# A selective-scan stage whose products with C are summed by accumulating transfers instead of by TensorE

## What is computed

```python
# layer 0
D = sum(adj, axis=1); d = (D + 1e-9) ** -0.5
x = x + relu(((adj * d[:, None] * d[None, :]) @ h) @ W.T + b)        # h = relu(layernorm(x))
# layer 1, after h = layernorm(relu(adj @ h @ gcn_w + gcn_b)) * ln_g + ln_b
dA  = exp(dt[:, :, None] * A[None])                   # (8192, 256, 16)
dBu = dt[:, :, None] * B[:, None, :] * u[:, :, None]
def step(hst, inp):
    dAt, dBut, Ct = inp
    hst = dAt * hst + dBut
    return (hst, hst @ Ct)                            # the sum over the 16 states
y = (ys + u * D_skip) * silu(z)
x = x + y @ w_out
```

## Time and profile before

| | us |
|---|---|
| median of 3 runs | 2683.72 |
| lowest, highest | 2681.23, 2686.16 |
| the profiled execution's own time | 2687.66 |
| its span in the profile | 2685.8 |

### The profile page before, as it was taken

How to read it: one execution, slowest core, us unless ns; L and a number is a source line. 1 busy time by engine, 2 the same in 40 slices (tenths; PEclk the granted TensorE clock), 3 DMA queues, 4 the chain that set the end, 5 groups by cost and what they waited for, 6 DMA issues and landing times.

```text
span 2685.8 us, 22298 instructions
## 1 busy us (share of the span) xinstructions
PE 2325.4 (87%) x7072; PEld 1314.6 (49%) x7072; DVE 2082.0 (78%) x2079; ACT 979.5 (36%) x1696; POOL 936.9 (35%) x409
## 2 busy tenths in 40 slices
PE   0347688999999999999999989999999989997776
PEld 0113344444447888888885444444444444443333
DVE  5888888886645666566652599999999899999997
ACT  0000000000004555555552455555545555555552
POOL 0000000000000000000000388777778788787554
PEclk9978789999999999999999999999999999998898
DMA  8999999898766555555547655555555555551121
GB/s 337 380 398 412 394 393 388 356 404 321 263 247 236 214 214 216 197 213 196 199 183 266 231 198 210 207 208 204 198 211 213 197 207 206 204 196 63 67 75 52
DMA packets 108325, 643.02 MB, mean 239 GB/s; under 512 B 14225, under 2 KB 15025, under 8 KB 42673
## 3 DMA queue, kind: packets, MB, share of 16 engines
q1 hardware_dynamic: 92160, 604.02, 59.3%
q10 hardware_dynamic: 16048, 37.57, 4.0%
HBM read 625.28 MB, written 16.25 MB: 239 GB/s over the span
## 4 chain that ended last, share of the span: by engine, by line
PE 57%; DVE 28%; issue 8%; ACT 3%; ACTq 1%; DMA 1%; DVEq 0%; POOL 0%; SPq 0%; POOLq 0%
PE ps L813 21%; PE ps L731 13%; DVE arena L550 11%; PE ps L853 10%; DVE arena L664 6%; DVE ps L653 6%; PE ps L890 4%; PE ps L928 4%; PE ps L753 2%; ACTq L958 1%; DMA diag_h<-adj 1%; PE ps L874 1%; PE ps L909 1%; DVE ring L664 1%; PE ps L932 1%
## 5 line engine op out<-in xcount | busy, mean ns | idle before, releaser
L813 PE MATMUL ps<-adj_parts,h_parts 128*128 128x512 f32 x2592 | 593.7, 391 | 2.5 <-ACT adj_parts L1024 2.2
L442 POOL TENSOR_TENSOR rstd<-base,minus_half 128x8 f32<-128x8 f32 (+1 forms) x40 | 84.7, 2118 | 1450.7 <-DVE base L490 877.9
L853 PE MATMUL ps<-ring,diag_h 128*128 128x512 f32 x1152 | 549.0, 611 | 0.3 <-DVE arena L640 0.2
L458 POOL TENSOR_TENSOR arena<-arena 128x1024 f32<-128x1024 f32 x192 | 458.5, 2394 | 251.1 <-ACT state L1091 251.1
L813 PEld LDWEIGHTS ps<-adj_parts,h_parts 128*128 128x128 f32 x2592 | 485.0, 188 | 108.6 <-ACT adj_parts L1024 4.7
L550 DVE TENSOR_TENSOR arena<-arena,ring 128x2048 f32<-128x2048 f32 x208 | 476.8, 2292 | 67.0 <-DMA ring<-adj 49.2
L731 PE MATMUL ps<-ring,arena 128*128 128x512 f32 x928 | 437.7, 633 | 62.4 <-DMA ring<-adj 62.4
L664 DVE TENSOR_TENSOR_SCAN arena<-arena,state,ps 128x512 f32<-128x512 f32 x384 | 470.6, 1267 | 26.1 <-DVE ps L653 1.0
L853 PEld LDWEIGHTS ps<-ring,diag_h 128*128 128x128 f32 x1152 | 223.8, 196 | 252.4 <-issue 249.3
L1099 ACT ACTIVATE arena<-arena,a_sb 128x512 f32<-128x512 f32 x512 | 338.3, 708 | 0.4
L577 DVE TENSOR_TENSOR adj_parts<-ring,adj_parts 128x1024 fp32r<-128x1024 f32 x216 | 264.0, 1224 | 94.3 <-ACT adj_parts L1024 83.5
(11 more groups left out here) (85 smaller groups left out, 1783.1 us busy)
## 6 DMA issues: line engine op xcount, KB each, us to landing
ring<-adj SPq DMA_DIRECT2D x480, 1024.0 KB, 6.5
arena<-c_scratch SPq DMA_DIRECT2D x128, 512.0 KB, 3.8
diag_h<-adj SPq DMA_DIRECT2D x32, 1024.0 KB, 12.2
arena<-x ACTq DMA_DIRECT2D x16, 512.0 KB, 4.7
x_scratch<-arena ACTq DMA_DIRECT2D x8, 512.0 KB, 3.0
arena<-x_scratch ACTq DMA_DIRECT2D x16, 256.0 KB, 4.3
out<-arena ACTq DMA_DIRECT2D x16, 256.0 KB, 3.0
lower_scratch<-arena ACTq DMA_DIRECT2D x7, 512.0 KB, 2.6
```

Of the source, the lines that this page charges most:

```text
L458: nc.gpsimd.tensor_tensor(buf, buf, c_row, ALU.mult).then_inc(mult_done, 1)
L813: last = nc.tensor.matmul(acc[:, c, :], h_parts[:, blk % 2, layer, h_part, a * F:(a + 1) * F], adj_parts[:, buf, adj_part, c * MM:(c + 1) ...
L853: last = nc.tensor.matmul((acc_c if i else y_ps)[:, c, :], tile_of(h1, JT * s + a), blk[:, a * STRIP + c * MM:a * STRIP + (c + 1) * MM], s ...
```

## The change

The sum over the 16 states no longer goes through PE pair by pair. There is a buffer y_pair of 128 x 2048 floats (two halves, y_sums[0] and y_sums[1]), paid for by two state buffers: HSB falls from 8 to 6, and the six lie as three pairs. In each chunk:

- POOL's products of slots 0 and 1 are written into y_pair, not in place. POOL waits before slot 0's for PE to have read the previous chunk's y_pair.
- After the product of slots 3, 5, 7, 9, 11 and 13, POOL issues a DMA with accumulate from the pair's buffers (128 x 2048 floats, 1 MB) onto y_pair. Before it issues one it waits for the previous one to have landed. POOL's own addition of pairs (L462 before) is gone.
- PE reads y_pair in slot 16 (the next chunk's slot 0) with four matmuls, after all six transfers have landed; in slot 18 it adds the last pair (slots 14 and 15) from the state buffers with four more. So there are 8 identity matmuls a chunk in all chunks, where there were 16 (32 in the last three).
- A scan that reuses a buffer waits for the product (pair 0), for the landing of its pair's transfer (pairs 1 to 6) or for PE's second sum (pair 7). The skip step on DVE waits for both sums.

```diff
-HSB = 8
+HSB = 6
-NSUM = 6
+YSUM, LAST_PAIR = 16, 18
-SPARED = 3
...
+        hs_pairs = [work2(2 * HALVES * T) for _ in range(HSB // 2 - 1)] + [ring[:, RING - 1, :]]
...
+        y_pair = work2(2 * HALVES * T)
...
+        def added(G):
+            k, p = divmod(G, PAIRS)
+            return 16 * ((PAIRS - 2) * k + min(max(p - 1, 0), PAIRS - 2))
...
-                    nc.gpsimd.tensor_tensor(buf, buf, c_row, ALU.mult).then_inc(mult_done, 1)
-                    if g % 2 and g // 2 < PAIRS_ADDED:
+                    k, n = divmod(g, DS)
+                    if n == 0 and k:
+                        pool.wait_ge(nsum_done, 2 * k - 1)
+                    nc.gpsimd.tensor_tensor(y_sums[n] if n < 2 else buf, buf, c_row, ALU.mult)\
+                        .then_inc(mult_done, 1)
+                    if n % 2 and 2 < n < DS - 2:
                         pool.wait_ge(mult_done, g + 1)
-                        even = hs[(g - 1) % HSB]
-                        nc.gpsimd.tensor_tensor(even, even, buf, ALU.add).then_inc(pair_done, 1)
+                        pool.wait_ge(y_added, added(g // 2))
+                        pool.dma_start(y_pair, hs_pairs[g // 2 % (HSB // 2)], accum_op=ALU.add)\
+                            .then_inc(y_added, 16)
...
-                        dve.wait_ge(nsum_done, (g - HSB) // 2 + 1)
+                        k_old, n_old = divmod(g - HSB, DS)
+                        if n_old < 2:
+                            dve.wait_ge(mult_done, g - HSB + 1)
+                        elif n_old < DS - 2:
+                            dve.wait_ge(y_added, added((g - HSB) // 2 + 1))
+                        else:
+                            dve.wait_ge(nsum_done, 2 * (k_old + 1))
...
+                k = chunk_at(g, YSUM)
+                if k is not None:
+                    pe.wait_ge(mult_done, DS * k + 2)
+                    pe.wait_ge(y_added, added(PAIRS * (k + 1) - 1))
+                    if k:
+                        pe.wait_ge(y_free, k)
+                    for j in range(2):
+                        for h in range(HALVES):
+                            last = nc.tensor.matmul(y_ps[:, h, :], ident[:, :], y_sums[j][:, h, :],
+                                                    start=j == 0, stop=False)
+                    last.then_inc(nsum_done, 1)
+                k = chunk_at(g, LAST_PAIR)
+                if k is not None:
+                    pe.wait_ge(mult_done, DS * (k + 1))
...
```

More of the change, by code:

```diff
@@ L236, in build @@
         da = [work2(HALVES, T) for _ in range(2)]
-        hs = [work2(HALVES, T) for _ in range(HSB - 2)]
-        hs += [ring[:, RING - 1, b * HALVES * T:(b + 1) * HALVES * T].rearrange("p (a b) -> p a b", a=HALVES)
-               for b in range(2)]
+        hs_pairs = [work2(2 * HALVES * T) for _ in range(HSB // 2 - 1)] + [ring[:, RING - 1, :]]
+        hs = [hs_pairs[b // 2][:, b % 2 * HALVES * T:(b % 2 + 1) * HALVES * T].rearrange("p (a b) -> p a b", a=HALVES)
+              for b in range(HSB)]
+        y_pair = work2(2 * HALVES * T)
+        y_sums = [y_pair[:, b * HALVES * T:(b + 1) * HALVES * T].rearrange("p (a b) -> p a b", a=HALVES)
+                  for b in range(2)]
         csb = [work2(2, T) for _ in range(2)]
@@ L336, in build @@
         mult_done = sem("mult_done")
-        pair_done = sem("pair_done")
+        y_added = sem("y_added")
         nsum_done = sem("nsum_done")
@@ L362, in evacuated @@
             eng.wait_ge(misc_free, misc_at[kind, k] + 1)
-        PAIRS_ADDED = (NCH - SPARED) * (DS // 2)
+        PAIRS = DS // 2
+        def added(G):
+            k, p = divmod(G, PAIRS)
+            return 16 * ((PAIRS - 2) * k + min(max(p - 1, 0), PAIRS - 2))
         weight_loads = [
@@ L700, in _ @@
                 if k is not None:
-                    dve.wait_ge(nsum_done, DS // 2 * (k + 1))
+                    dve.wait_ge(nsum_done, 2 * (k + 1))
                     if k:
@@ L875, in _ @@
                                      start=True, stop=True).then_inc(b_ready, 1)
-                G, odd = divmod(g - NSUM, 2)
-                if not odd and 0 <= G < NCH * DS // 2:
-                    pair = G % (DS // 2)
-                    terms = [hs[2 * G % HSB]]
-                    if G < PAIRS_ADDED:
-                        pe.wait_ge(pair_done, G + 1)
-                    else:
-                        pe.wait_ge(mult_done, 2 * G + 2)
-                        terms.append(hs[(2 * G + 1) % HSB])
-                    if pair == 0 and G:
-                        pe.wait_ge(y_free, G // (DS // 2))
-                    for j, term in enumerate(terms):
-                        for h in range(HALVES):
-                            last = nc.tensor.matmul(y_ps[:, h, :], ident[:, :], term[:, h, :],
-                                                    start=pair == 0 and j == 0,
-                                                    stop=pair == DS // 2 - 1 and j == len(terms) - 1)
+                k = chunk_at(g, YSUM)
[5 more added lines that the diff above has]
+                    for j in range(2):
+                        for h in range(HALVES):
+                            last = nc.tensor.matmul(y_ps[:, h, :], ident[:, :], y_sums[j][:, h, :],
[4 more added lines that the diff above has]
+                    pe.wait_ge(mult_done, DS * (k + 1))
+                    for j in range(2):
+                        for h in range(HALVES):
+                            last = nc.tensor.matmul(y_ps[:, h, :], ident[:, :],
+                                                    hs[(DS * k + DS - 2 + j) % HSB][:, h, :],
+                                                    start=False, stop=j == 1)
                     last.then_inc(nsum_done, 1)
```

## The result

The changed kernel takes 2858.72 us (median of four runs, 2857.6 to 2859.83) against 2683.03 before: ratio 1.0652, 95% interval 1.0635 to 1.0669. It is 176 us slower; the prediction was +61 (2745 us). The time lies inside the stated range of 2652 to 2880, near its upper end. The profiled execution has a span of 2857.9 us, 172 above that of before.

The account below looks back on a forecast made before the run. DVE was taken as the floor mid-stage, held above it by waits for PE. -35 (PE) + 90 (new wait) + 6 (end) = +61 on 2687.66 gave 2749, which lay 3.9 above the median: 2745 us, range 2652 to 2880.

Parts of the forecast that it names:

- The landing, x = 10.5: x, from the end of a pair's second product to its accumulation's landing, issue included: two passes 8.7 plus 1.8 for load.
- The row of transfers: Each accumulation waits for the one before; PE in slot 16 waits 8.9 us, DVE stalls 7.5 a chunk, +90.
- The second condition: Sixth landing at 1833.23 + 5x, from pair 2's products; governs from x = 9.4; PE's wait is 5x - 43.6.
- Rival A: Transfers land in time, x below 9.4: 2664 us; the skill's pages' estimate, 6.8, would make it hold; chance 0.38.
- Rival C: DMA engines full or adding itself slow, x above 12.5: at 14 about 2980 us; sign: scans wait for y_added; chance 0.12.
- The relief, -35 us: DVE's waits for PE's pick and output product go as three sums leave slots 4 to 9: -35.2 us, 2.9 a chunk.
- The sum of 3.44 us in the middle: PE's four matmuls on y_pair in slot 16, taken as 3.44 us; with it PE does 5.65 against DVE's 3.73.
- rival D: PE idles more and its granted clock falls: a microsecond a chunk at most; only narrows Rival A, no separate chance.
- The end, +6: After product 13 of the last chunk: landing 8.7, then 16 rows of PE 8.7; +6 us, between +1 and +8.
- POOL's additions were hidden: nothing gained: 104 additions of 2.35 us taken off POOL were hidden, since POOL waits for ACT before its products: nothing gained.
- Six buffers cost nothing: A scan reusing a buffer comes about three and a half slots after the pair's products; up to 12.5 us cost nothing.
- Last three chunks nothing: No pass C there, x about 8.7, PE hides more than it needs, DVE hardly waited before: nothing either way.

Follow-up runs that it names:

- experiment 3: The changed kernel with only a quarter of each pass C block loaded from strip 2 on: 2762.31 us.
- experiment 4: The changed kernel with accumulating transfers of half the size, one slab of each pair left out (also called the half-size kernel): 2753.41 us.
- experiment 7: The changed kernel with two accumulators, for even and odd pairs, the second in a block of pass C's ring; five transfers a chunk: 2830.25 us.
- experiment 1: The changed kernel without its accumulating transfers and the waits of POOL and PE for them: 2618.34 us.
- Experiment 6: The changed kernel with sixteen matmuls, results not used, on PE ahead of its wait for the sixth transfer: 2862.94 us.
- 17: The kernel before without POOL's additions of pairs, PE summing every product: 2770.22 us.
- 18: The kernel with three of six transfers, the additions of pairs 4 to 7 given to PE: 2728.84 us, ratio 1.0158 to the kernel before.

## Why the prediction was right and wrong

**The landing, x = 10.5: near, in part by luck.** It is 10.7 in the chain shown, issue included, and 11.05 in the mean of eleven rows (10.5 to 11.6). The two passes are there in engine time, but a copy takes 9.6 in full rows, so the second pass is worth 1.5 us of a link and not 2.8. Three quarters of the loads are worth 2.0 (experiment 3), near the 1.8 allowed for load. The base of 8.7 for an undisturbed accumulation agrees with the 8.1 and 8.5 us, median, between 2640 and 2760, where pass C has ended, with 0.5 for the issue. Its parts are not borne out: at the prediction's 1.4 us for each 0.5 MB that passes, half the bytes would land 2.8 us sooner, and they did 1.7 us sooner (experiment 4).

**The row of transfers: right.** The second condition governs (pair 2 + 5x), a DMA stands before PE's sum in slot 16, and in eleven of the twelve chunks DVE has one long wait for the pick of slot 18, 7 to 15 us. Rival A (lands in time) and its lower price of 6.8 are out: 6.9 us is the fastest of the 96 landings, and the median is 9.6. Rival C (full queues) is partly right, and the prediction could not tell it from its own case, since it compared means: the engines are full inside the row, and scans wait for landings, 66 us in the twelve chunks, which was a sign of C; yet x stayed under the 12.5 that it asked for. It takes over with two accumulators (experiment 7), where C loads and one accumulation, not the row, are on the chain.

**The relief, -35 us: the first step that failed.** It was taken off each chunk although the new wait governs the chunk. By its terms the prediction leaves 74.0 - 2.9 - 43.6 - 1.4 = 26.1 us from the last landing to pair 2's products; the runs show 32.4. In the loop shown above this stretch is PE's own unbroken work, late from the sum on, and what is saved elsewhere does not shorten it. What PE saved in slots 4 to 9 ends up as waiting for the landing, 12.8 us in the mean where the prediction has 8.9. A term may be credited only while its stretch is on the path: the relief is worth 62 us without transfers (experiment 1), and with six no part of it shows. That is 2.9 us a chunk. This share is worked out from the chain; no run has six transfers without the relief.

**The sum of 3.44 us in the middle: mis-sized.** PE waits 10 to 16 us for the landing, and its four matmuls then take 6.3 us in the mean (6.70 at a granted clock of 0.55 in the chunk shown), 2.8 more. The prediction counted this at the program's end and nowhere else, and in rival D called the clock worth a microsecond at most. Experiment 6 gets 1.8 of it back.

**Together:** the prediction's chunk was 74.0 - 2.9 + 7.5 = 78.6. Add 2.9 for the relief, 5 x 0.55 = 2.8 for x and 2.8 for the sum: 87.1. The rows begin 87.6 us apart, and the twelve chunks took 87.35 in the mean; half a microsecond is left over. 87.35 - 78.6 is 8.75 a chunk, 105 us of the 115 that the prediction was short; 5 more lie at the end and 3 in the two chunks before it. By the chunk marks one chunk, 2271.09 to 2368.38, took 97.3 us and the next 82.7, but the rows begin 87.2 and 89.7 us apart there:

```profile
2230.43 12.44 DMA arena<-arena
...
2317.66 14.51 DMA arena<-ring
...
2407.35 11.87 DMA arena<-arena
```

So what is late is mainly the mark, on DVE, which waited in that chunk for another load as well. Why one landing takes 7.4 us and another 14.5 in this stretch stays open.

```profile
DVE arena L653 <- DMA arena<-upper_scratch: 7.3, 1, 7.3
```

**The end, +6: mis-sized.** +11.3. The prediction let one landing of 8.7 us stand behind product 13 there. Accumulations in the last chunk still land in 7 to 8.8 us each with pass C's loads gone, and five of them in a row reach the end of the program, with PE's sum at 6.70 behind them; these are the last two:

```profile
2823.47 7.06 DMA arena<-ring
2830.57 0.49 issue
2831.08 6.95 DMA arena<-arena
2838.03 0.09 issue
2838.11 6.70 PE ps L903 x8
```

**"POOL's additions were hidden: nothing gained": wrong, without effect here.** POOL itself had time, but DVE's short instructions take longer or shorter as POOL's fall (experiments 1, 17 and 18); in the changed kernel DVE is off the path, and it pays nothing.

**Six buffers cost nothing:** right where it was meant. From before the step costs 7 us by one run each, none of it in the twelve chunks. In the changed kernel scans waited for landings 53.4 and 21.0 us over the run, in time that the row takes anyway. **Last three chunks nothing:** right, 2.8 us for the two before the last.

## What to carry to other kernels

A row of transfers that each wait for the one before is a path of its own: add up its links, and the work between its end and its next start, and compare that with the loop before crediting any engine with a relief. While the row governs, removing one link pays that link in every turn of the loop (159 us for the sixth, against 40 by an even share); with few links little is left to gain (23 us from three to two, 5 from two to one). So try fewer links before other cures. And look at where in the loop an engine is late: the kernel without a transfer, whose main difference is that two sums are moved out of those slots, is 1.2% faster than the one before.

## What the hardware showed

Halving an accumulation to 0.5 MB shortened its median landing only from 9.6 to 7.9 us. An accumulation of 1 MB never landed in under 6.9 us, though a copy's fastest in mid-stage took 4.6. Issuing one held POOL for 0.88 us, a copy 0.59.

A DVE instruction with two inputs in SBUF can be held up by POOL's work. The 40x512 subtraction takes 0.69 us in each of its 16 runs of experiment 1; where two products of POOL ran back to back beside it (1874.58 to 1879.52), it took 5.78 us, and stood in the chain of the half-size kernel:

```profile
1874.30 5.78 DVE parts L709
```

The Trainium skill has this rule in SBUF — State Buffer, section "SBUF: two separate sides": whichever of GpSimd and such a VectorE instruction starts first keeps the shared port pair for its whole duration, and the other is blocked. The trace agrees that one is held up, and adds that it can last over two of POOL's instructions: DVE ended 0.56 us behind the second. On who started first it does not fit as it stands, since DVE's start is recorded 0.28 us ahead of the first product's.
